# Gated cross-attention block on one core: context statistics over ScalarE's queue, and a DMA transpose in the output stage

## What is computed

```
lat = layer_norm(_layernorm(x), ln_lat_g, ln_lat_b)
ctx = layer_norm(context, ln_ctx_g, ln_ctx_b)
q = lat @ Wq                      # per head
k, v = split(ctx @ Wkv)           # per head
k = apply_rope(k, cos, sin)
attn = softmax(clip(q k^T * DHEAD**-0.5, -11, 11))
x = x + tanh(g_xattn) * ((attn v) @ Wo + bo)
...
lhs = _layernorm(x)
q_lhs = clip(round(lhs / lhs_scale), -127, 127)     # lhs_scale: row maximum / 127
q_rhs = clip(round(rhs / rhs_scale), -127, 127)     # rhs_scale: column maximum / 127
x = x + tanh(g_ffn) * (q_lhs @ q_rhs * lhs_scale * rhs_scale)
```

## Time and profile before

| | |
|---|---|
| median of 3 runs | 1479.47 us (1477.96 to 1479.47) |
| the profiled execution, its own time | 1478.47 us |
| its span, first to last instruction | 1476.7 us, 22445 instructions |
| mean granted TensorE clock | 0.990 |
| busy: TensorE, VectorE, ScalarE, GpSimd | 1444.3, 1268.0, 705.0, 101.8 us |
| projections | to about 470 us |
| attention | to 1356.7 us |
| output stage | from 1356.7 us to the end |

### The profile page before, as it was taken

The page is one execution under the profiler, slowest core; times in us unless marked ns, Lnnn a source line. Parts: engine busy times, 40 slices in busy tenths (PEclk is TensorE's granted clock), DMA queues, the critical chain, the costliest instruction groups (busy, mean ns, idle before and its releaser), DMA issues. The chain is left out here.

```text
span 1476.7 us, 22445 instructions
## 1 busy us (share of the span) xinstructions
PE 1444.3 (98%) x7938; PEld 872.4 (59%) x7938; DVE 1268.0 (86%) x1112; ACT 705.0 (48%) x821; POOL 101.8 (7%) x66
## 2 busy tenths in 40 slices
PE   8988999999999999999999999999999999999997
PEld 7866888888887444444444444444444444444774
DVE  6746878778774999999999999999999999996987
ACT  4422222222232665665656556565565656654342
POOL 0400000000000000000000000000000000001775
PEclk9998999999999999999999999999999999999998
DMA  8786777677667445541551551551452452403552
GB/s 278 262 240 234 258 261 225 223 249 239 242 196 248 113 102 185 137 109 44 136 127 26 135 128 32 133 127 38 122 128 47 111 128 56 103 16 94 156 165 86
DMA packets 156992, 219.22 MB, mean 148 GB/s; under 512 B 39697, under 2 KB 89873, under 8 KB 149777
## 3 DMA queue, kind: packets, MB, share of 16 engines
q1 hardware_dynamic: 153792, 213.35, 49.4%
q10 hardware_dynamic: 3152, 5.25, 1.0%
HBM read 133.70 MB, written 84.84 MB: 148 GB/s over the span
## 5 line engine op out<-in xcount | busy, mean ns | idle before, releaser
L1158 ACT ACTIVATE prob<-score_ps 128x1024 f32<-128x1024 f32 x512 | 483.0, 1032 | 198.7 <-PE score_ps L1105 198.7
L1117 PE MATMUL value_ps<-prob,v_st 128*64 128x512 f32 x2048 | 467.7, 598 | 1.0 <-DVE prob L1200 1.0
L1216 DVE TENSOR_TENSOR prob_sum<-prob_sum,prob 128x2048 f32<-128x2048 f32 x192 | 440.1, 2292 | 13.5
L1105 PE MATMUL score_ps<-q_st,k_st 64*128 64x512 f32 x3072 | 394.5, 402 | 2.2 <-PEq L112 2.1
L1105 PEld LDWEIGHTS score_ps<-q_st,k_st 64*128 64x128 f32 x3072 | 271.3, 184 | 173.7 <-issue 105.6
L1200 DVE TENSOR_SCALAR prob<-prob 128x4096 f32<-128x4096 f32 x128 | 292.6, 2286 | 41.3 <-ACT prob L1158 39.1
L1117 PEld LDWEIGHTS value_ps<-prob,v_st 128*64 128x64 f32 x2048 | 135.6, 136 | 267.6 <-issue 265.4
L873 DVE TENSOR_TENSOR k_cos<-k_raw,rope 128x1024 f32<-128x1024 f32 x32 | 39.2, 1224 | 64.3 <-ACT k_raw L702 64.3
L1525 POOL MEMSET unround<- 128x1 f32 x1 | 0.1, 98 | 1281.7 <-POOLq L122 1281.7
L702 ACT ACTIVATE k_raw<-proj_ps 128x1024 f32<-128x1024 f32 x31 | 31.9, 1029 | 111.9 <-PE proj_ps L245 111.9
L711 ACT ACTIVATE v_out<-proj_ps 128x1024 f32<-128x1024 f32 x31 | 31.9, 1030 | 110.5 <-PE proj_ps L245 110.5
(11 more groups left out here) (125 smaller groups left out, 1320.3 us busy)
## 6 DMA issues: line engine op xcount, KB each, us to landing
k_st<-k_scr SPq DMA_DIRECT2D x128, 256.0 KB, 6.2
k_scr<-k_hi SPq DMA_DIRECT2D x64, 256.0 KB, 2.9
v_scr<-v_out SPq DMA_DIRECT2D x32, 512.0 KB, 3.8
k_scr<-k_lo SPq DMA_DIRECT2D x64, 256.0 KB, 4.4
q_st<-q_scr SPq DMA_DIRECT2D x16, 1024.0 KB, 10.6
v_st<-v_scr SPq DMA_DIRECT2D x16, 1024.0 KB, 13.5
q_scr<-q_hi SPq DMA_DIRECT2D x32, 256.0 KB, 5.2
q_scr<-q_lo SPq DMA_DIRECT2D x32, 256.0 KB, 4.7
```

Source lines behind the costliest of these rows:

```text
L1105: last = pe.matmul(score_ps[:, u % BANKS, a, :], k_st[slot][rows, k_part, s * P:(s + 1) * P], q_st[slot][rows, q_part, cols], start=(t == ...
L1117: last = pe.matmul(value_ps[rows, :], v_st[slot][:, s, rows], prob[:, b % 2, i, a * CH:(a + 1) * CH], start=(s == 0), stop=(s == STEPS - 1))
L1158: act.activation(prob[:, b % 2, u % BATCH_UNITS, :], score_ps[:, u % BANKS, :, :], ACT.Exp, scale=SCALE).then_inc(exped, 1)
L1216: dve.tensor_tensor(total, total, halves[j], ALU.add).then_inc(added, 1)
```

## The change

**Statistics of context chunk 0.** The store of the statistics and the two loads of `rows` leave SP's program and enter ScalarE's: `store_first_stats` after `q_hi` of (2, 7), `spread_first_stats` after `q_hi` of (3, 0). `store_scales` and `load_inverses` move to ScalarE as well, after `q_hi` of (2, 4) and (2, 5). VectorE's `normalise_columns(0, 0)` moves from (3, 1) to (3, 2), `tok_split` of chunk 0 from (3, 3) to (3, 5), `wo_low(0)` from (3, 6) to (3, 7); ScalarE's `affine_columns(0, 0)` from (3, 3) to (3, 4). The later chunks keep their order.

**Output stage.** TensorE's four transposes per tile, their PSUM tile and ScalarE's copy `y_qt` go. Instead ScalarE, right after `y_int`, waits until that is complete and issues a DMA transpose from `y_int` to `y_qt` in SBUF. TensorE's product waits for its landing (`turned_in`). All turns are now written out; the hardware loop is gone.

```diff
@@ projections, SP @@
             sp.wait_ge(stat_stored, 16 * (c + 1))
-            if isinstance(c, int) and c == 0:
-                sp.wait_ge(tok_lo_made, QCH)
...
-                if (n, m) == (2, 7):
-                    spread_stats(0, 0, 0)
-                if (n, m) == (2, 4):
-                    store_scales()
-                if (n, m) == (2, 6):
-                    load_inverses()
@@ projections, ScalarE @@
+        def store_first_stats():
+            act.wait_ge(ctx_rstd_made, 1)
+            act.dma_start(stat_scr[0:2, :].rearrange("f (p t) -> p f t", t=CT), stat[:, 0, :, :]).then_inc(stat_stored, 16)
+
+        def spread_first_stats():
+            act.wait_ge(stat_stored, 16)
+            act.wait_ge(tok_lo_made, QCH)
+            for f in range(2):
+                act.dma_start(rows[:, 0, f, :], stat_scr[f:f + 1, :].broadcast_to((P, CH))).then_inc(rows_in[0], 16)
...
-                if m == 3 and n + 1 == QCH:
+                if (n, m) == (2, 4):
+                    store_scales()
+                if (n, m) == (2, 5):
+                    load_inverses()
+                if (n, m) == (2, 7):
+                    store_first_stats()
+                if (n, m) == (3, 0):
+                    spread_first_stats()
+                if (n, m) == (3, 4):
                     affine_columns(0, 0)
@@ projections, VectorE @@
-                if n + 1 == QCH and m == 6:
+                if n + 1 == QCH and m == 7:
                     wo_low(0)
-                if n + 1 == QCH and m == 7:
                     rhs_integers(0)
...
-                if m == 1 and n + 1 == QCH:
+                if m == 2 and n + 1 == QCH:
                     normalise_columns(0, 0)
-                if m == (4 if n == 0 else 3):
+                if m == (4, 3, 3, 5)[n]:
                     tok_split(n + 1, slot, tok if n + 1 < QCH else ctok[0])
@@ output, all engines @@
-        for t in range(PEELED):
-            turn(t, [(t - k) % 2 for k in range(DEPTH + 1)])
-        with eng.Fori(PEELED // 2, TILES // 2) as i:
-            for j in range(2):
-                turn(2 * i + j, [(j - k) % 2 for k in range(DEPTH + 1)])
-        for t in range(TILES, TILES + DEPTH):
+        for t in range(TILES + DEPTH):
             turn(t, [(t - k) % 2 for k in range(DEPTH + 1)])
@@ output, TensorE @@
-            if there(t - 3):
-
-                s = slots[3]
-                pe.wait_ge(int_made, t - 2)
-                if not first(t - 3, 2):
-                    pe.wait_ge(qt_copied, t - 4)
-                for k in range(KT):
-                    last = pe.transpose(turn_ps[:, s, k, :], y_int[:, s, k * P:(k + 1) * P], ident_bf[:, :])
-                last.then_inc(int_turned, 1)
-            if terms:
                 pe.wait_ge(o_lo_made, t)
                 attend(range(2 * OT, 3 * OT)).then_inc(attended, 1)
             if there(t - 3):
 
-                pe.wait_ge(qt_copied, t - 2)
+                s = slots[3]
+                pe.wait_ge(turned_in[s], 16 * ((t - 3) // 2 + 1))
@@ output, ScalarE @@
-            if there(t - 3):
-                s = slots[3]
-                act.wait_ge(int_turned, t - 2)
-                if not first(t - 3, 2):
-                    act.wait_ge(multiplied, t - 4)
-                act.activation(y_qt[:, s, :, :], turn_ps[:, s, 0:KT, :], ACT.Copy).then_inc(qt_copied, 1)
             if there(t - 2):
                 s = slots[2]
                 act.wait_ge(chain, CHAIN * (t - 1))
                 if not first(t - 2, 2):
-                    act.wait_ge(int_turned, t - 3)
+                    act.wait_ge(turned_in[s], 16 * ((t - 2) // 2))
                 act.activation(y_int[:, s, :], y_clip[:, :], ACT.Identity, bias=unround[:, 0:1]).then_inc(int_made, 1)
+                if not first(t - 2, 2):
+                    act.wait_ge(multiplied, t - 3)
+                act.wait_ge(int_made, t - 1)
+                act.dma_start_transpose(y_qt[:, s, :, :], y_int[:, s, :]).then_inc(turned_in[s], 16)
```

More of the change, by code:

```diff
@@ L125, in flamingo_kernel @@
         with ExitStack() as stage:
-            output(nc, stage, x, o_scr, out, late, ends, gate_tanh, ident_bf, eps_col)
+            output(nc, stage, x, o_scr, out, late, ends, gate_tanh, eps_col)
 class Ready:
@@ L463, in load_rhs_column @@
             sp.dma_start(rhs_col[:, :], rhs_t.rearrange("(p t) k -> p t k", t=KT)[:, i, :]).then_inc(rhs_col_in, 16)
[L465 to L472, removed]
         def load_piece(i, wo_row, rhs_row):
@@ L646, in affine_columns, with store_scales, load_inverses @@
                                scale=gains[:, 2, k:k + 1]).then_inc(affine_made, 1)
+        def store_scales():
+            act.wait_ge(rhs_inv_made, 1)
+            act.dma_start(ready.scale_scr.rearrange("f (p t) -> p f t", t=KT), rhs_scales[:, :, :]
+                          ).then_inc(ready.scale_stored, 16)
+        def load_inverses():
+            act.wait_ge(ready.scale_stored, 16)
+            act.dma_start(inv_row[:, :], ready.scale_scr[1:2, :].broadcast_to((P, DIM))).then_inc(inv_row_in, 16)
+        def store_first_stats():
[6 more added lines that the diff above has]
+                act.dma_start(rows[:, 0, f, :], stat_scr[f:f + 1, :].broadcast_to((P, CH))).then_inc(rows_in[0], 16)
         def wo_high(i):
@@ L681, in _ @@
                     affine(n + 1)
-                if m == 3 and n + 1 == QCH:
+                if (n, m) == (2, 4):
[7 more added lines that the diff above has]
+                if (n, m) == (3, 4):
                     affine_columns(0, 0)
-                if m == 5 and n + 1 == QCH:
+                if (n, m) == (3, 5):
                     wo_high(0)
@@ L1231, in _, with output @@
         all_pairs(dve, pair)
-def output(nc, ctx, x, o_scr, out, late, ends, gate_tanh, ident_bf, eps_col):
+def output(nc, ctx, x, o_scr, out, late, ends, gate_tanh, eps_col):
     sb, ps, sem = tools(nc, ctx)
@@ L1238, in output @@
     DEPTH = 5
-    PEELED = TPB
     LAST = ALLPAIRS - 1
@@ L1262, in output @@
     wo_ps = ps("wo_ps", [P, 2, DIM])
-    turn_ps = ps("turn3_ps", [P, 2, 2 * KT, P], BF16)
     ffn_ps = ps("ffn_ps", [P, 2, DIM])
@@ L1278, in output @@
     int_made = sem("int_made")
-    int_turned = sem("int_turned")
-    qt_copied = sem("qt_copied")
+    turned_in = [sem(f"turned_in{i}") for i in range(2)]
     multiplied = sem("multiplied")
```

## The result

| | before | changed |
|---|---|---|
| median of the runs | 1478.8 us (1477.96 to 1479.47, 6 runs) | 1491.91 us (1490.32 to 1493.37, 6 runs) |
| ratio to before | | 1.0091, 95% interval 1.0078 to 1.0103 |
| span of the profiled execution | 1476.7 us | 1489.4 us |

What follows compares the result with a forecast made beforehand. TensorE, busy 98% of the span, was taken as the bound. Front -10.0, output turns +3.3 and tail +1.4 sum to -5.3 us, from the median 1474.2 us; range 1468 to 1486.

Steps and rivals of the forecast that it cites:

- I take 0.4, since the nearest row is one plain issue of this engine: Output stage, ScalarE: issuing the transpose takes 0.4 us, with bounds 0 and 1.4; a plain issue takes 0.35.
- my 6.73: Output stage: VectorE's turn grows from 5.98 to 6.73 us, longer than TensorE's 6.43.
- The first rival: Output stage: the transpose's issue holds ScalarE's queue 0.9 us or more; 1485.2 us at the 1.4 bound; chance 0.27.
- The chain of the turn: Output stage, from `x_mid`: `y_int`, transpose, store, `o_hi`, `std`, hand-offs, together 3.05 us to VectorE's reciprocal, against 2.30.
- The last two turns: Output stage's end: the last turn up to the last tile's `x_mid` takes 5.98 us, without `o_hi`.
- The tail: From the last `y_int` to the last product: a DMA landing of 2.7 us plus 0.05, +1.4 us (bounds +0.7 and +3.3).
- In the turns before it is hidden: Output stage before the tail: the transpose's landing fits into two turns, 13.46 us, so it may take 6.2 us.
- The front: Projections: earlier statistics of context chunk 0 start the first K group at 115.0, gaining 10.0 us (bounds 11.9 and 4.5).
- I take 5.0, near the first, since the 8.2 were spent behind q stores of the same queue: Projections: the 4 KB statistics store on ScalarE's queue takes 5.0 us, between bounds of 4.4 and 8.2.
- Then the rows take 5.8 us as before: Projections: the row loads take 5.8 us (bounds 4.5 and 8.1) and land at 101.7.
- my third rival: Projections: the rows don't come earlier, DMA engines being busy; rows at 107.2, K group at 120.5, 1479.7 us; chance 0.15.
- the last sentence of the prediction: Projections: the forecast is wrong on the front if the first K group starts after 120.

Runs made afterwards that it cites:

- the kernel with the late issue: Changed kernel, but ScalarE issues each tile's transpose one turn later, behind `o_hi` and `std`: 1476.21 us, ratio 0.9983.
- the two kernels with a free ScalarE: Changed kernel with the transpose issued one turn later on ScalarE, 1476.21 us, and changed kernel with it issued by SyncE, 1475.26 us.
- the early columns: Changed projections with the output stage of before, plus chunk 0's 1 MB column load issued two groups earlier: 1472.05 us, ratio 0.9958.
- the small q stores: Changed projections, old output stage, chunk 0's columns loaded earlier, plus most of the q stores of groups 18 to 25 put off: 1477.68 us in one run.

## Why the prediction was wrong

**The place was right, the size of one term was not.** "I take 0.4, since the nearest row is one plain issue of this engine" is the step that failed. The issue of the transpose takes 1.21 us, near the upper bound of 1.4 in the same paragraph. The store behind it takes 0.59 where I put 0.35. Together that is 1.05 of the 1.10 us by which the turn, 7.83, exceeds my 6.73. In my own sum, 12 turns of 1.05 more make 3.3 + 12.6 = 15.9 us from turn 4 to turn 17, and 15.7 were measured; that it fits so closely is partly luck, since three shorter turns and a longer last one about cancel. (For 12 turns 0.1 us of issue time is worth 1.2 us, not the 1.1 that I wrote; with it the upper bound of that stretch is 15.3, not 14.3.) The first rival (the issue holds ScalarE, 1485.2 us at 1.4) was the case that came true; its condition, 0.9 us, was met.

**The chain of the turn** held link by link: `y_int` to 0.84 (0.83 predicted), then the two issues, `o_hi` 1.06, `std` 0.28, reciprocal. VectorE's turn is 5.98 us, and longer by as much as the reciprocal starts later than 2.30 us after `x_mid`. Three kernels show it: with the reciprocal at 4.15, 3.52 and 5.43 us their turns are 7.83, 7.21 and 9.11. In the kernel with the late issue it starts at 1.61, and the turn is TensorE's 6.36.

**The last two turns.** I put the turn into turn 17 at 5.98 us, because it has no `o_hi`; it took 6.83. And the stretch from `x_mid` of turn 17 to the last `y_int` is in my sum at nothing, without a reason; its `std` too stands behind a transpose and a store: +1.1 us.

**The tail** was right: +1.2 against +1.4. The product behind the last transpose starts 2.5 us after its issue, not the 5.2 that I estimated besides for four blocks in a row. "In the turns before it is hidden" was right as well: the landings of 2.3 to 5.7 us lie under the 6.2 us that I allowed. The allowance does not hold in the early turns, where TensorE is less far ahead, as the two kernels with a free ScalarE show.

**The front** brought 4.4 us, just outside the bounds of 11.9 and 4.5. Of my 10.0 us, 5.9 were to come from the rows' earlier landing and 4.2 from the work behind it; measured are 0.1 and 4.3. The failed step is the store of the statistics: "I take 5.0, near the first, since the 8.2 were spent behind q stores of the same queue". It was 9.9. I had read the 8.2 as a matter of the queue; the runs show that it is a matter of the engines' load. The move to another queue took the store into a busier stretch, a mean DMA share of 1.04 from 89.6 to 99.4 against 0.72 from 93.5 to 101.7 before, and made it longer. A second step failed beside it: "Then the rows take 5.8 us as before". They took 8.0, and that is my third rival: the rows at 107.2 and the K group at 120.5, where 107.4 and 120.6 were measured. By the last sentence of the prediction, too, I was wrong on the front. Everything behind the landing held: 13.2 us from VectorE's start to the K group (107.43 to 120.60), 13.3 predicted. With the changed projections alone, with the early columns, with the small q stores and with SyncE's transposes it is 13.2 us again. In the kernel with the small q stores the landing was at 101.99 and the K group at 115.18, the 101.7 and 115.0 of the prediction, by other parts: 2.3 us for the store, and 10.0 for the rows.

**Sum.** -4.4 for -10.0, +14.9 from the first `x_mid` to that of turn 17 for +3.3, and +1.1 for nothing: these make 18 us of error, against 1474.2. Rivals 1 and 3 came together. The range took in the bounds one at a time, but not both at their bad ends, which gives -4.5 + 14.3 + 1.4 = +11.2, and that is nearly what came.

**The rule on issue time.** The measured 1.21 us is per DMA at both widths. The Trainium skill ("DMA: Bandwidth & Descriptors", "Why a DMA increments its semaphore by 16 and not by 1") gives, for earlier generations, 512 cycles for a plain DMA and, from SBUF to SBUF, 262,144 for 8,192 transposed tiles, which is 32 for each. My estimate from it was 0.7 us; it leaned the right way, but the trace does not agree with its size. Nor do the runs show a part that grows with the tiles, since half the columns cost the same.

## What to carry to other kernels

Price the issue of a DMA as an instruction of the engine that issues it, and of a kind that no trace shows, take the upper bound when the engine has 0.2 us of slack. Here the transpose's 1.21 us and the store's 0.59 put the reciprocal 1.85 us later; 0.69 of that went into the gap between VectorE's turn and TensorE's, and 1.16 into each full turn, 7.83 us for 6.67. The same DMA issued by SyncE cost nothing. A small transfer that stands on the critical path is not made faster by another queue when the engines behind all queues are full; look at the DMA share of the stretch into which it moves, and clear that stretch. Compare a gain with what stands in front of it: the rows for which the statistics were moved came 0.1 us earlier, and the 4.4 us came from the order of the work behind them. And read a long wait of the bounding engine together with who else is late: most of TensorE's 24.5 us for transposes was a symptom.

## What the hardware did that I had not expected

- A DMA transpose holds the issuing engine 1.21 us on ScalarE and 1.19 us on SyncE (medians of 16), and 1.27 us at half the columns (median of 32).
- The plain store issued right behind it takes 0.59 us (median of 15), and 0.34 when it stands ahead of it.
- The same 4 KB store takes 2.3 us with the DMA engines at a share of 0.22 and 7.6 to 10.1 us with them full (five kernels), on ScalarE's queue, where one load of 256 KB is its only predecessor still under way.
- A transpose of 128x512 in bf16 lands 2.3 to 5.7 us after its issue on ScalarE with the median at 3.2, 2.3 to 4.1 (median 2.4) when ScalarE issues it a turn later, and 2.3 to 3.7 (median 2.4) on SyncE.
